# Reordering half a batch of a fused attention and mixture-of-adapters kernel: the router logits of the second half behind the third group's gate and up products, the down products in another order, and VectorE's row statistics in four pieces

## The reference

```python
h = _layernorm(x) * (1 + ca) + sa
x = x + ga * attention(h)
h = _layernorm(x) * (1 + cb) + sb
x = x + gb * ffn(h)

# ffn
gate_base, up_base = xf @ Wg.T, xf @ Wu.T                 # 256 -> 704
base_out = silu(gate_base) * up_base @ Wd.T
probs = softmax(xf @ Wr.T)                                # 8 experts
topw, topi = top_k(probs, 2)
for each expert e:
    g_lora, u_lora = xf @ Ag_e.T @ Bg_e.T * 2, xf @ Au_e.T @ Bu_e.T * 2   # rank 16
    h = silu(gate_base + g_lora) * (up_base + u_lora)
    acc += (h @ Ad_e.T @ Bd_e.T * 2) * weight_e
out = base_out + acc
```

## Time and profile before

| | |
|---|---|
| median of 3 runs | 688.92 us (688.87 to 689.52) |
| the profiled execution | 688.73 us |
| its span, first to last instruction | 686.9 us |
| TensorE busy | 652.9 us, 95% |
| TensorE weight loads busy | 558.8 us, 81% |
| VectorE busy | 474.2 us, 69% |
| GpSimd busy | 377.4 us, 55% |
| ScalarE busy | 356.7 us, 52% |
| TensorE's mean granted clock | 0.994 of full speed |

### The profile page before, as it was taken

How to read it: one execution, slowest core, us unless ns; L and a number is a source line. 1 busy time by engine, 2 the same in 40 slices (tenths; PEclk the granted TensorE clock), 3 DMA queues, 4 the chain that set the end, 5 groups by cost and what they waited for, 6 DMA issues and landing times.

```text
span 686.9 us, 10710 instructions
## 1 busy us (share of the span) xinstructions
PE 652.9 (95%) x3772; PEld 558.8 (81%) x3772; DVE 474.2 (69%) x1146; ACT 356.7 (52%) x642; POOL 377.4 (55%) x473
## 2 busy tenths in 40 slices
PE   4869999999999999999999999999999999999996
PEld 3559987888879987888878897798888998788885
DVE  5997678478886677658976767747987657637323
ACT  4635455546455546465455446564454546654543
POOL 3785345538577236647576516654765635543644
PEclk9989999999999999999999999999999999999999
DMA  8300020000000020000000001000000000000000
GB/s 311 122 1 1 1 62 0 1 2 31 0 2 31 1 62 0 1 1 32 0 1 32 1 1 62 0 1 18 15 1 1 32 1 1 0 1 1 31 0 32
DMA packets 14054, 15.45 MB, mean 22 GB/s; under 512 B 1328, under 2 KB 12720, under 8 KB 14000
## 3 DMA queue, kind: packets, MB, share of 16 engines
q1 hardware_dynamic: 14000, 14.76, 6.4%
HBM read 10.57 MB, written 4.19 MB: 21 GB/s over the span
## 4 chain that ended last, share of the span: by engine, by line
PE 82%; DVE 12%; issue 2%; POOL 2%; DMA 1%; ACT 1%; DVEq 0%; SPq 0%
PE ps L1263 76%; PE ps L1272 6%; DVE xr L856 2%; DVE hid L1103 1%; DVE rstd L829 1%; DVE zb L844 1%; DMA xs<-in_L_attn_x 1%; DVE xT_lo L890 1%; POOL ring_lo L469 1%; DVE mv L836 1%; DVE tr_full L856 1%; ACT act_s L709 1%; DVE zb L927 0%; DVE stat L841 0%; DVE nr_a L827 0%
## 5 line engine op out<-in xcount | busy, mean ns | idle before, releaser
L469 POOL TENSOR_TENSOR ring_lo<-hid,ring_hi 128x512 fp32r<-128x512 f32 x144 | 189.3, 1319 | 115.9 <-ACT ring_hi L717 115.2
L1103 DVE TENSOR_TENSOR hid<-act_s,ps 128x512 f32<-128x512 f32 x120 | 81.9, 684 | 82.0 <-ACT act_s L709 81.4
L709 ACT ACTIVATE act_s<-ps 128x512 f32<-128x512 f32 x120 | 71.7, 597 | 123.0 <-PE ps L1263 122.4
L717 ACT ACTIVATE ring_hi<-hid 128x512 fp32r<-128x512 f32 (+1 forms) x144 | 90.3, 627 | 16.2 <-DVE hid L1101 8.7
L461 POOL TENSOR_TENSOR xT_lo<-tr_full,xT_hi 128x512 fp32r<-128x512 f32 x28 | 35.9, 1297 | 33.5 <-ACT xT_hi L588 33.5
L1263 PE MATMUL ps<-wdT_hi,ring_hi 128*128 128x256 f32 x192 | 53.6, 285 | 0.0
L1263 PE MATMUL ps<-wdT_lo,ring_hi 128*128 128x256 f32 x192 | 53.2, 282 | 0.0
L1263 PE MATMUL ps<-wdT_hi,ring_lo 128*128 128x256 f32 x160 | 45.2, 282 | 0.0
L1263 PE MATMUL ps<-tm_hi,bgT_hi 128*128 128x512 f32 x96 | 39.5, 411 | 5.7 <-DVE hid L1103 5.7
L1263 PE MATMUL ps<-vv_hi,pT_hi 128*128 128x256 f32 x144 | 43.3, 301 | 0.0
L476 POOL TENSOR_TENSOR xr<-xr,y_gb 128x256 f32<-128x256 f32 x31 | 22.1, 739 | 34.2 <-DVE y_gb L1138 34.2
(11 more groups left out here) (229 smaller groups left out, 2026.4 us busy)
## 6 DMA issues: line engine op xcount, KB each, us to landing
xs<-in_L_attn_x SPq DMA_DIRECT2D x4, 1024.0 KB, 5.6
out<-xr SPq DMA_DIRECT2D x7, 512.0 KB, 3.0
s_mod<-in_L_wmod SPq DMA_DIRECT2D x1, 1024.0 KB, 8.8
s_qkvT<-in_L_attn_qkv SPq DMA_DIRECT2D x1, 768.0 KB, 10.3
s_wg<-in_L_ffn_Wg SPq DMA_DIRECT2D x1, 704.0 KB, 7.4
s_wu<-in_L_ffn_Wu SPq DMA_DIRECT2D x1, 704.0 KB, 8.6
s_wd<-in_L_ffn_Wd SPq DMA_DIRECT2D x1, 640.0 KB, 7.3
s_mod<-in_L_wmod SPq DMA_DIRECT2D x1, 512.0 KB, 6.9
```

Source lines behind the costliest of these rows:

```text
L469: pool.tensor_sub(ring[1][:, place(n), :], hid[:, n % HID, :], ring[0][:, place(n), :].bitcast(fp32)).then_inc(h_lo.sem, 1)
L709: nc.scalar.activation(act_s[:, n % 2, :], ps[:, 2 * (n % 2), :], ACT.Silu).then_inc(silu_ready.sem, 1)
L717: nc.scalar.activation(ring[0][p0:P, place(n), :], hid[p0:P, n % HID, :], ACT.Copy).then_inc(h_hi.sem, 1)
L1103: V.tensor_mul(hid[:, n % HID, :], act_s[:, n % 2, :], ps[:, 2 * (n % 2) + 1, :]).then_inc(h_ready.sem, 1)
```

## The change

Four things. TensorE makes both gate and up products of group 2 (`base(ci, g, 1)` too) ahead of `logits(1)`. The first half's down products have a list written out, `DOWNS`: experts of groups 0 and 1, then the base path of group 1 and of group 0, then group 2; the last ones of a group now go by `FILL` too. With the list, other ring slots are freed at other places, so the waits of the two spreading steps are worked out by `freed`, and ScalarE's `spread_weights(1)` goes behind the two `adapter_input_high`. VectorE's statistics are cut into four pieces, behind `hid` of units 2, 3, 4 and 5.

```diff
+        def downs(g, slots):
+            return [(g, slot, a) for slot in slots for a in range(2)]
+        DOWNS = (downs(0, (1, 2)) + downs(1, (1, 2)) + downs(1, (0,)) + downs(0, (0,)) + downs(2, (0, 1, 2)),
+                 downs(0, (0, 1, 2)) + downs(1, (0, 1, 2)) + downs(2, (0, 1, 2)))
...
+        def freed(ci, slots):
+
+            return max(down_position(n) for n in range(ci * UPC, (ci + 1) * UPC) if place(n) in slots)
...
-                        act.wait_ge(h_used.sem, h_used.at(b, down_position(unit(ci - 1, GROUPS - 1, 1, 1))))
+                        act.wait_ge(h_used.sem, h_used.at(b, freed(ci - 1, (RING - 2, RING - 1))))
...
-                        spread_weights(1)
                         adapter_input_high(1, 0)
                         adapter_input_high(1, 1)
+                        spread_weights(1)
                         dsum_high(0)
...
+            def newton(lo, n, rounds):
 
                 v, a, y = nr_v[:, lo:lo + n], nr_a[:, lo:lo + n], rstd[:, lo:lo + n]
-                link(guess(lo, n))
-                for _ in range(NEWTON):
+                for _ in range(rounds):
                     link(V.tensor_mul(a, y, y))
                     link(V.scalar_tensor_tensor(a, a, -0.5, v, ALU.mult, ALU.mult))
                     link(V.scalar_tensor_tensor(y, a, 1.5, y, ALU.add, ALU.mult))
...
-                        dve.wait_ge(h_used.sem, h_used.at(b, down_position(unit(ci - 1, GROUPS - 1, 1, 1))))
+                        dve.wait_ge(h_used.sem, h_used.at(b, freed(ci - 1, (RING - 4,))))
...
                     hidden(r)
-                    if r == 5:
+                    if r == 2:
                         x1_stats(TC + 3)
+                    if r == 3:
                         moments(range(TC, NT))
                         mark(V.tensor_scalar(neg_mean[:, TC:NT], mv[:, TC:NT, 0], -1.0, None, ALU.mult))
-                        rsqrt(TC, TC)
+                    if r == 4:
+                        link(guess(TC, TC))
+                        newton(TC, TC, 1)
+                    if r == 5:
+                        newton(TC, TC, NEWTON - 1)
                         dve.sem_inc(norm_ready.sem, 1)
                         V.tensor_mul(shift[:, TC:NT], neg_mean[:, TC:NT], rstd[:, TC:NT]).then_inc(rstd_ready.sem, 1)
...
-                FILL = {(0, 0): (0, 0, 0, 0), (0, 1): (0, 1, 1, 1), (0, 2): (2, 2, 2, 1),
-                        (1, 0): (0, 0, 0, 0), (1, 1): (1, 2, 1, 1), (1, 2): (1, 2, 1, 1)}
+                FILL = {(0, 1): (0, 1, 1, 1, 1), (0, 2): (2, 2, 2, 1, 1),
+                        (1, 1): (1, 2, 1, 1, 1), (1, 2): (1, 2, 1, 1, 1)}
...
                         if g:
                             base(ci, g, 0)
+                            base(ci, g, 1)
                         if ci == 0 and g == 2:
                             logits(1)
-                        if g:
-                            base(ci, g, 1)
```

More of the change, by code:

```diff
@@ L280, in half_unit @@
             return unit(ci, GROUPS - 1, slot, 1)
-        def down_order(ci, g):
-            slots = (0, 1, 2) if ci or g else (1, 2, 0)
-            return [(slot, a) for slot in slots for a in range(2)]
+        def downs(g, slots):
+            return [(g, slot, a) for slot in slots for a in range(2)]
+        DOWNS = (downs(0, (1, 2)) + downs(1, (1, 2)) + downs(1, (0,)) + downs(0, (0,)) + downs(2, (0, 1, 2)),
+                 downs(0, (0, 1, 2)) + downs(1, (0, 1, 2)) + downs(2, (0, 1, 2)))
         def down_unit(q):
-            ci, g, rest = q // UPC, q % UPC // 6, q % 6
-            slot, a = down_order(ci, g)[rest]
+            ci, rest = divmod(q, UPC)
+            g, slot, a = DOWNS[ci][rest]
             return unit(ci, g, slot, a)
@@ L829, in rsqrt @@
                     link(V.scalar_tensor_tensor(y, a, 1.5, y, ALU.add, ALU.mult))
+            def rsqrt(lo, n):
+                link(guess(lo, n))
+                newton(lo, n, NEWTON)
             def moments(tiles):
@@ L1476, in down @@
                     if slot == 0:
-                        if j == 0 and ci == 0:
+                        first = (g, slot, a) == next(d for d in DOWNS[ci] if d[1] == 0)
+                        if first and ci == 0:
                             pe.wait_ge(shifted_ready.sem, shifted_ready.at(b, 1))
-                        elif j == 0:
+                        elif first:
                             pe.wait_ge(wmask_ready.sem, wmask_ready.at(b, 3))
@@ L1483, in down @@
                                 last_mm = mm(ps[:, 6 + t // 2, t % 2 * D:(t % 2 + 1) * D], hn[ph][:, t * P:(t + 1) * P], wdT[pw][:, j, :],
-                                             j == 0 and t % 2 == 0 and (ph, pw) == (0, 0), False)
+                                             first and t % 2 == 0 and (ph, pw) == (0, 0), False)
                     else:
@@ L1537, in units @@
                                         transposes(b, KT * NC + KT + k, 6 + k, k, [zb[:, tile, :] for tile in range(TC, NT)])
-                                count = FILL[ci, g][(slot - 1) * 2 + a]
-                                for f in fill[:count]:
-                                    down(*f)
-                                fill = fill[count:]
+                                downs_before(g, (slot - 1) * 2 + a)
                                 if g == 0 and a == 1:
@@ L1551, in units @@
                                 adapters(ci, g, slot, a)
-                        keep = KT if ci == 0 and g == 1 else 0
-                        for f in fill[:len(fill) - keep]:
-                            down(*f)
-                        fill = fill[len(fill) - keep:]
+                        downs_before(g, 4)
                 def last_downs(ci):
-                    return [(ci, GROUPS - 1, s, a) for s, a in down_order(ci, GROUPS - 1)]
+                    return [(ci, *d) for d in DOWNS[ci][-6:]]
                 pe.wait_ge(weight_lo, LATE)
```

11 lines of the change are left out of this document (7 added, 4 removed).

## The result

The changed kernel takes 693.47 us (median of 6 runs, 693.32 to 693.93) against 688.92 us before: a ratio of 1.0064 (95% interval 1.0051 to 1.0077), 4.55 us slower by the medians. The prediction was 690.2 us with a range of 687.0 to 693.0, so it lies 3.3 us too low and the range ends 0.5 us short. The profiled execution took 693.44 us (span 691.6, TensorE's mean granted clock 0.991); against the 688.73 us of the one before that is +4.71. Of this, 0.25 us lies ahead of the first batch's mask products (they start at 92.89 before and at 93.14 after), in front of everything that the change touches; from 28 to 32 us TensorE's granted clock was 0.60 in this profile and 1.00 in the one before.

What follows compares the result with a forecast made beforehand. TensorE, 82% of the span, was taken to bound the kernel, with its wait for `hid` of unit 6 the target. Terms -0.44 - 0.30 + 0.30 + 1.72 = +1.28 on 688.73, plus 0.19 for the median: 690.2 us, range 687.0 to 693.0.

Steps and rivals of the forecast that it cites:

- The pieces up to unit 8: Statistics in four pieces: TensorE loses 0.25 us at unit 6, 0.82 + 0.10 at unit 7; unit 8's wait shrinks.
- piece 4: VectorE's statistics behind unit 5: sixth instruction held by GpSimd's `ring_lo` to about 269.69, unit 8 at 270.70 against 270.81.
- I take -0.11 us a batch: Net effect of the statistics in four pieces on TensorE up to unit 8: -0.44 us in all.
- Logits: Second half's logits moved behind the group's base products: their low input is there in time, -0.30 us in three batches.
- The -0.10: TensorE's step ahead of the second half's logits, about 0.10 us too long in three batches, becomes normal.
- Downs in another order: 0: First half's down products: ring positions up to the eleventh reached at the same time or sooner, no TensorE wait, 0 us.
- `pick_er`: ScalarE's `pick_er` behind both `xT_hi` delays `tm_hi` by 0.66 us; first `bdT` matmul waits: +0.43 us a batch, +1.72.
- Unit 15: TensorE waits for `hid` of unit 13, delayed by the logits' move: +0.10 us in three batches, +0.30.
- The rival in which unit 13's `hid` is caught in its middle: Late `ring_lo` of unit 12 holds `nr_v`'s followers: 0.98 us lost in three batches, 692.8 us; chance 0.10.
- The rival of the cheap small instructions: Piece 3's seven VectorE instructions fit before `ring_lo`, unit 7 doesn't stall: gain 5.75 us, 684.9 us; chance 0.18.
- piece 3: VectorE's statistics behind unit 4: held twice by GpSimd's `ring_lo`, so `hid` of unit 5 starts at about 266.85, not 264.55.
- +1.28: Sum of the predicted terms for the whole kernel, in us: -0.44 - 0.30 + 0.30 + 1.72.

Runs made afterwards that it cites:

- pick_last: Changed kernel with `pick_er` one place later, behind dsum's rounding (`tm_hi`) instead of ahead of it: 691.09 us, ratio 1.0033.
- newton_only: Kernel before with row statistics behind unit 2, means behind 3, first guess behind 4, Newton steps and shift on GpSimd: 694.42 us, ratio 1.0096.

## Why the prediction was wrong, by its own steps

**The pieces up to unit 8: right.** Unit 6 lost 0.14 + 0.11 (0.25 predicted), unit 7 0.83 + 0.11 (0.82 + 0.10). `nr_v` lasted 0.98 us, `nr_a` 1.21, and the sixth instruction of piece 4 was held to 271.24. Units 6 to 8 together lost 1.39 where unit 8 alone had lost 1.60: -0.21 a batch, where -0.11 was summed. The exclusive hold was read rightly from the earlier trace rows.

**The step that failed: "I take -0.11 us a batch".** It closed the statistics' account at unit 8. I assumed that behind unit 8 every engine is shifted alike. It isn't, since TensorE's stall moved from unit 8 to unit 7. (All the moves named here contain the 1.63 us by which the second batch begins later (252.58 to 254.21); the differences between them count.) The silu of unit 7 now comes late, and behind it on ScalarE stand the copy of unit 6 and two normalising instructions, so that the silu of unit 8 moved from 272.51 to 274.35, 1.84 later, while TensorE's unit 8 moved by 1.43 (270.81 to 272.24). VectorE follows ScalarE: `hid` of unit 9 and `gated` moved by 1.83. GpSimd's `ring_lo` of unit 9 follows a silu that TensorE sets, and moved by 1.45 (277.79 to 279.24). The difference of 0.38 us turned a lead of 0.24 into a lag, and the write takes 1.02 us more: 0.41 at unit 12 and 0.51 at unit 13, 2.76 us in three batches. Moving the write alone gave back 2.72 (693.47 to 690.75); delaying it alone, in the kernel before, brought the collision and its chain; with the write in place but unheld (the statistics put back) neither unit waited. That the difference of 0.38 comes from ScalarE's queue is read from the rows and was not tried by itself.

The Trainium skill (page "SBUF — State Buffer", section "Who interferes with whom"), which the prediction cites, has a rule for this too: a VectorE instruction with two SBUF inputs contends with a GpSimd instruction that reads SBUF, and the port pair that they share is an exclusive lock. The write reads two SBUF operands, and the traces agree: in the fourteen kernels profiled here it takes 0.68 to 0.71 us or 1.70 to 1.77 us, and nothing in between. I had applied the rule to the instructions that the change moves, and not to those that it makes late.

**Logits: right in sign, far off in worth.** The -0.10 was there. What I priced at 0.30 is 4.6 us once `xT_lo` is late, since the logits otherwise wait 1.10 us in three batches and bring the clock down. The move is insurance, not a gain: within the change it keeps the collision from costing what it costs in the kernel before.

**"Downs in another order: 0": right as a wait, wrong as a verdict.** No down waited. But without the order, the moved logits hold up the next base down by 1.26 us, and with it `pick_er` must move. The three edits are one: the logits need the down order (bank 7), the down order needs `pick_er` behind the inputs (ring places), and that costs 0.54 us ahead of `bdT`.

**`pick_er`: mechanism right, size 0.43 against 0.54.** I let it start 0.50 us behind the second `xT_hi`; it started 0.62 behind (310.30 to 310.92), and the missing 0.11 is that. In four batches it is 2.16 in place of 1.72; `pick_last` gave back 2.38.

**Unit 15: 0.24 in place of 0.10.** It waits as much with the statistics in one block, so it belongs to the logits' move. The rival in which unit 13's `hid` is caught in its middle did not come.

**The rival of the cheap small instructions.** It failed as the rows had said: seven of them took 3.1 us in piece 3 (265.36 to 268.47, two of them held), and an unheld one takes 0.16. The prediction set it against 58 cycles, 0.065 us. The same section of the Trainium skill (page "VectorE: DVE Perf Modes", on the TRN2 errata) says that this row under-predicts and puts the measured fixed term at about 150 cycles; with four elements that is an estimate of 0.16 us, and the traces agree with that value.

The sum: +1.28, and -0.40 for the statistics, +0.42 for unit 15, +0.44 for `pick_er`, +2.76 for units 12 and 13, makes +4.50, against +4.55 measured.

## What to carry to other kernels

Where two engines exclude each other, list every pair of instructions that passes with less room than the change will shift them by, as far as the end of the stage and not only to the next stall; a lead of 0.24 us was worth 6 us. Move an instruction that may be held to where its engine waits anyway: it is held as long, and costs nothing. When edits come together, price each with the others undone as well, since one of no gain of its own may be what makes another possible.

## What the hardware showed that I had not expected

TensorE's granted clock fell in the middle of a busy kernel. Outside the first 46 and the last 6 us of the kernel it fell to 0.50 for about 3.4 or 6.8 us (1.5 to 1.6 or 3.1 us lost, by TensorE's starts) only where a stall of 1.1 to 1.3 us stood directly ahead of or behind the sixteen small logit products; in the change, where unit 13's 0.40 us stands six products ahead of them, it stayed at 1.00 in all four batches. It did not come each time: once in three batches with such a wait in the profile of the statistics alone, three times in four in one of those with the old down order. A stall of 1.50 us among 512-column products, as at unit 8 before, never brought it.

The number of spells seems to differ from run to run. The runs of three of those kernels spread over 3 to 5 us, those of the kernels without such a stall over less than 1.2. The mean granted clock of each run is on record and goes with it: with the statistics alone the longest run, 698.36 us, had 0.985 and the shortest, 693.63, had 0.989; in `newton_only` the two longest, 697.16 and 697.86, had 0.983 and 0.985 and the other four 0.990. Where in a run the clock fell, only the profiled ones show.
